# Cross-attention and quantised FFN on one core: one pass of scores with a block-transposed row maximum, and a new order of the attention step

## What is computed

```python
def xattn(q, kv, Wq, Wk, Wv, Wo, bo):        # 8 heads of 32
    qh, kh, vh = split_heads(q @ Wq), split_heads(kv @ Wk), split_heads(kv @ Wv)
    scores = einsum('bqhd,bkhd->bhqk', qh, kh) * 32 ** -0.5
    attn = softmax(scores, axis=-1)
    return merge_heads(einsum('bhqk,bkhd->bqhd', attn, vh)) @ Wo + bo

def ffn(x):                                   # weights rounded to -1, 0, 1, rows to 8 bits
    h = bitlinear(layernorm(x, g1, b1n), w1, b1)       # 256 -> 1024
    h = gelu(h, approximate=False)
    return bitlinear(layernorm(h, g2, b2n), w2, b2)    # 1024 -> 256

x = x + xattn(layernorm_plain(x), ctx_768, Wq, Wk, Wv, Wo, bo)
x = x + ffn(layernorm_plain(x))
```

## Time and profile before

| | |
|---|---|
| median of 3 runs | 1164.03 us (1163.67 to 1164.55) |
| the profiled execution | 1168.3 us, its span 1166.6 us |
| busy share of the span | TensorE 87%, its weight loads 63%, VectorE 88%, ScalarE 71%, GpSimd 60% |
| granted TensorE clock, mean | 0.982 |
| HBM | 90 GB/s over the span |

### The profile page before, as it was taken

How to read it: one execution, slowest core, us unless ns; L and a number is a source line. 1 busy time by engine, 2 the same in 40 slices (tenths; PEclk the granted TensorE clock), 3 DMA queues, 4 the chain that set the end, 5 groups by cost and what they waited for, 6 DMA issues and landing times.

```text
span 1166.6 us, 34313 instructions
## 1 busy us (share of the span) xinstructions
PE 1019.7 (87%) x12163; PEld 732.0 (63%) x12209; DVE 1024.2 (88%) x1589; ACT 833.6 (71%) x2147; POOL 701.0 (60%) x924
## 2 busy tenths in 40 slices
PE   5999999999999999999999876777777777777775
PEld 4777777777777777777777533444444444444444
DVE  1588989988888888888889899999999999999996
ACT  3555655676656666666665566999999999999993
POOL 3345555754545555555556546777777777777776
PEclk8999999999999999999999978999999999999997
DMA  5556867667788766676565400332222333333334
GB/s 140 138 144 158 151 148 153 146 144 144 152 141 131 162 147 151 144 143 142 142 141 121 115 25 19 37 37 36 36 36 36 36 36 37 36 36 38 38 37 68
DMA packets 144483, 114.30 MB, mean 98 GB/s; under 512 B 51580, under 2 KB 134908, under 8 KB 144408
## 3 DMA queue, kind: packets, MB, share of 16 engines
q1 hardware_dynamic: 126824, 96.38, 38.2%
q0 software_dynamic: 16864, 16.26, 11.7%
q10 hardware_dynamic: 720, 0.66, 0.2%
HBM read 71.23 MB, written 33.63 MB: 90 GB/s over the span
## 4 chain that ended last, share of the span: by engine, by line
PE 49%; DVE 23%; issue 20%; DMA 3%; ACT 2%; SPq 1%; POOL 1%; DVEq 1%; another core or an unknown queue 0%; ACTq 0%; POOLq 0%
PE banks L1317 8%; PE banks L1304 8%; DVE gn_low L797 6%; DVE gn_high L797 6%; PE banks L1236 6%; PE banks L1281 5%; PE banks L1247 5%; PE banks L1256 4%; PE banks L1267 3%; DMA r_rows<-x_r 2%; PE banks L1269 2%; DVE gn_high L783 2%; DVE gn_low L783 2%; PE banks L1295 2%; PE banks L1270 1%
## 5 line engine op out<-in xcount | busy, mean ns | idle before, releaser
L977 ACT ACTIVATE probs<-banks 120x512 f32<-120x512 f32 x256 | 132.2, 602 | 87.2 <-PE banks L1286 87.2
L517 POOL TENSOR_TENSOR f_r<-f_ve,neg_half 128x2 f32<-128x2 f32 x62 | 43.8, 707 | 211.9 <-DVE f_ve L734 210.3
L689 DVE TENSOR_REDUCE nm_part<-banks 128x16 f16<-128x1920 f32 x64 | 138.1, 2157 | 35.1 <-PE banks L1236 34.8
L1020 ACT ACTIVATE g_dev<-g,g_sum 128x1024 bf16<-128x1024 f32 x128 | 149.0, 1164 | 0.0
L1025 ACT ACTIVATE g<-banks,h_dq 128x1024 f32<-128x1024 f32 x128 | 142.5, 1130 | 8.4 <-PE banks L1183 8.4
L1201 PE MATMUL banks<-w_t,g_t 128*128 128x256 bf16 x1008 | 123.2, 276 | 13.5 <-ACT g_t L1052 10.9
L1317 PE MATMUL banks<-wo_sb,o_t 128*128 128x256 f32 x512 | 128.2, 394 | 5.8 <-DVE o_t L831 5.8
L1201 PEld LDWEIGHTS banks<-w_t,g_t 128*128 128x128 f16 x1008 | 94.7, 98 | 51.9 <-issue 30.3
L1304 PE MATMUL banks<-xt,wq_c 128*128 128x256 f32 x512 | 126.2, 389 | 0.6 <-issue 0.6
L1177 PE MATMUL banks<-w_t,h_t 128*128 128x512 bf16 x466 | 116.3, 385 | 5.5 <-ACT g L1025 1.9
L1317 PEld LDWEIGHTS banks<-wo_sb,o_t 128*128 128x128 f32 x512 | 94.4, 195 | 24.5 <-DVE o_t L831 6.2
(11 more groups left out here) (165 smaller groups left out, 2715.6 us busy)
## 6 DMA issues: line engine op xcount, KB each, us to landing
x_in<-in_x SPq DMA_DIRECT2D x64, 256.0 KB, 4.1
xt<-in_x_t SPq DMA_DIRECT2D x64, 256.0 KB, 3.7
xr<-in_x SPq DMA_DIRECT2D x64, 256.0 KB, 5.7
out<-xr SPq DMA_DIRECT2D x64, 256.0 KB
out<-res POOLq DMA_DIRECT2D x62, 256.0 KB, 4.4
r_bc<-r_rows SPq DMA_DIRECT2D x64, 128.0 KB, 4.8
ctx_t<-in_ctx_t SPq DMA_DIRECT2D x64, 120.0 KB, 3.2
w_raw<-in_w_t SPq DMA_DIRECT2D x8, 256.0 KB, 5.8
```

The lines of the kernel that those rows point to most:

```text
L689: dve.tensor_reduce(nm_part[:, q, :, 0:T * C], s_p, AX.X, ALU.max, negate=True).then_inc(max_done, 1)
L977: act.activation(probs[:, p, j, :, :], sc_p[:, j, :, :], ACT.Exp, scale=SCALE).then_inc(probs_done, 1)
L1020: act.activation(g_dev[:, t, :], g[:, p, t, :], ACT.Square, scale=-float(F), bias=g_sum[:, p, t:t + 1], accum_out=g_ssq[:, p, t:t + 1]).th ...
```

## The change

It touches the attention stage on all engines and the tail.

- `maxima` is gone. `scores(i)` is computed once, with the keys on the partitions, and no shift at first. The keys are padded from 120 to 128 by repeating eight of them (`KP`), so that all 128 partitions hold scores; only the first `KV = 120` go on.
- `largest(i)`: VectorE takes the negative maximum over transposed 32 by 32 blocks of all four banks (128 x 2048 in, 128 x 64 out). That leaves four partial maxima of each row, one for each 32 keys. `turn_minima` transposes them, VectorE takes the least of the four (`nm_row`) and spreads it over a block-diagonal tile (`nm_t`, 128 x 256).
- `shift(i)`: 8 products of 256 columns (f16) add the shift to the scores that still stand in the banks. ScalarE then takes the exponentials. ScalarE's copy of the minima is gone, and the exponentials come in two halves with `high_half` between them.
- The projection `y_p` moves from bank 0 to bank 2, which it shares with keys and queries; `project` runs a step later (block i-2).
- All four engines have a new order in the step; keys and values are copied at the start of ScalarE's step, and `q_t` stands before `o_t` at the end of VectorE's.
- All 64 steps run through `attn`, and the hand-written tail is shorter. The sum over the weights (`w2s_p`) moves to bank 3 and into step NB-2.

The core of the diff (semaphore and shape declarations, the tail of ScalarE and the input's padding are left out):

```diff
-        y_p = bank[0].rearrange("p (t n) -> p t n", t=T)
+        y_p = bank[2].rearrange("p (t n) -> p t n", t=T)
...
@@ VectorE
+                def largest(b):
+                    after(dve, nmt_ps, b)
+                    dve.wait_ge(raw_ps, b + 1)
+                    dve.tensor_reduce(nm_part[:, :, 0:C * RB], blocks_p, AX.X, ALU.max, negate=True,
+                                      apply_transpose=True).then_inc(max_done, 1)
...
+                    b = i - 3
+                    (f_r_done, h_centred; the two affine instructions, h_affine)
+                    if isinstance(i, int) and i == -1:
+                        largest(0)
+                    elif live(i, NB) and not (isinstance(i, int) and i == 0):
+                        largest(i)
+                    (h_max of block i-3)
+                    b = i
+                        dve.wait_ge(nmt_ps, b + 1)
+                        dve.tensor_reduce(nm_row[:, :], nmt_p.rearrange("p (k r) -> p r k", r=32), AX.X, ALU.min).then_inc(min_done, 1)
+                    (h_cl of block i-3)
+                        after(dve, sc_ps, b)
+                        dve.wait_ge(min_done, b + 1)
+                        dve.tensor_tensor(nm_t[:, :, :], nm_row[:, :].unsqueeze(1).to_broadcast([P, RB, 32]),
+                                          block_sel[:, :].unsqueeze(2).to_broadcast([P, RB, 32]), ALU.mult).then_inc(nmt_done, 1)
+                    (xr of i-2, h_qs of i-3, reciprocal of i-1, statistics of i-2, split of i-1,
+                     aggregate, centre with f_ve behind its first half, of i-2; q_t of i+2; o_t of i-1)
...
@@ ScalarE: attn(i, n)
+                    if live(i + 1, NB):
+                        copy_keys_values(i + 1, q, (n + 1) % 4)
+                    if live(i - 1, NB):
+                        copy_o(i - 1, q)
+                    (row sums and squares of block i + 4)
+                        exponentials(i, p, range(0, HC // 2))
+                        high_half(i - 1, q)
+                        exponentials(i, p, range(HC // 2, HC))
+                        cast_rows(i - 4, n % 4)
...
@@ TensorE
+                def scores(b, p):
+                    after(pe, probs_done, 4 * b)
+                    pe.wait_ge(q_done, b + 1)
+                    pe.wait_ge(k_done, b + 1)
+                    for c in range(C):
+                        for j in range(HC):
+                            last = pe.matmul(sc_p[:, j, c, :], k_t[strip(j), p, c, :], q_t[strip(j), p, c, :],
+                                             start=(c == 0), stop=False, skip_group_check=True)
+                    last.then_inc(raw_ps, 1)
+                def turn_minima(b):
+                    after(pe, o_done, b)
+                    pe.wait_ge(max_done, b + 1)
+                    pe.transpose(nmt_p, nm_part[:, :, :].rearrange("p j n -> p (j n)"), ident_h[:, :]).then_inc(nmt_ps, 1)
+                def shift(b):
+                    pe.wait_ge(nmt_done, b + 1)
+                    for c in range(C):
+                        for j in range(HC):
+                            last = pe.matmul(sc_p[:, j, c, :], head_sel[strip(j), c, :],
+                                             nm_t[strip(j), :, :].rearrange("p b r -> p (b r)"),
+                                             start=False, stop=(c == C - 1), skip_group_check=True)
+                    last.then_inc(sc_ps, 1)
...
                 def keys_values(b, p):
                     after(pe, q_done, b)
                     after(pe, v_done, b)
+                    (first product of the values)
+                    after(pe, x1_done, b - 3)
                     (products of the keys, rest of the values)
...
                 def attn(i, n):
-                    maxima(i + 1); values(i - 1); sums(i - 1); keys_values(i + 2); scores(i)
-                    spread_inverses(i - 1); queries(i + 2); turn_minima(i + 1); project(i - 1)
+                    scores(i); values(i - 1); project(i - 2); turn_minima(i); sums(i - 1); shift(i)
+                    keys_values(i + 2); queries(i + 2); spread_inverses(i - 1)
...
@@ tail
-                steps(dve, A0, NB - 1, L0, L1, attn, 4, aside)
-                affine_h(NB - 4); add_y(NB - 3); statistics(NB - 3); centre_h(NB - 3); invert(NB - 2); split(NB - 2); weigh(NB - 2)
-                centre(0); add_y(NB - 2); ffn(0); invert(NB - 1); statistics(NB - 2); split(NB - 1); affine_h(NB - 3); centre_h(NB - 2)
-                centre(1); weigh(NB - 1); ffn(1); add_y(NB - 1); statistics(NB - 1); affine_h(NB - 2); centre_h(NB - 1)
-                ffn(2); affine_h(NB - 1); ffn(3)
+                steps(dve, A0, NB, L0, L1, attn, 4, aside)
+                affine_h(NB - 3); invert(NB - 1); split(NB - 1); centre(0); add_y(NB - 2); weigh(NB - 1)
+                statistics(NB - 2); centre_h(NB - 2); ffn(0); centre(1); affine_h(NB - 2); add_y(NB - 1)
+                ffn(1); statistics(NB - 1); centre_h(NB - 1); ffn(2); affine_h(NB - 1); ffn(3)
```

More of the change, by code:

```diff
@@ L684, in attn @@
                         dve.tensor_tensor(xr[:, r2, :, :], y_p, xr[:, r2, :, :], ALU.add).then_inc(x1_done, 1)
[L685 removed]
+                    b = i - 3
                     if live(b, NB):
[L687 to L689 removed]
+                        dve.wait_ge(h_clipped, b + 1)
+                        dve.reciprocal(h_qs[:, q, :], h_cl[:, q, :]).then_inc(h_scaled, 1)
                     b = i - 1
@@ L724, in attn @@
                         last.then_inc(x1_aggr, 1)
+                        after(dve, hq_cast, b - 3)
+                        dve.wait_ge(x1_aggr, b + 1)
+                        for t in range(T):
+                            last = dve.scalar_tensor_tensor(out=h[:, r2, t, :], in0=xr[:, r2, t, :],
+                                                            scalar=f_mv[:, p, t, 0:1], in1=g1_bc[:, :],
+                                                            op0=ALU.subtract, op1=ALU.mult)
+                            if t == 0:
+                                dve.tensor_scalar(f_ve[:, p, :], f_mv[:, p, :, 1], 1.0 + LN_EPS, LN_EPS * LN_EPS,
+                                                  ALU.mult, ALU.add).then_inc(f_ve_done, 1)
+                        last.then_inc(h_centred, 1)
+                    b = i + 2
+                    if live(b, NB):
+                        after(dve, raw_ps, b - 1)
+                        dve.wait_ge(r_loaded[p], (b - p) * 8 + 16)
+                        dve.wait_ge(kvq_ps, b + 1)
+                        dve.tensor_tensor(q_t[:, p, :, :].rearrange("p m (t n) -> p m t n", t=T),
+                                          q_p.rearrange("p m (t n) -> p m t n", t=T),
+                                          r_bc[:, p, :].rearrange("p (n t) -> p t n", t=T).unsqueeze(1).to_broadcast([P, C, T, P]),
+                                          ALU.mult).then_inc(q_done, 1)
                     b = i - 1
@@ L741, in attn @@
-                    b = i - 2
-                    if live(b, NB):
-                        after(dve, hq_cast, b - 3)
-                        for t in range(T):
-                            last = dve.scalar_tensor_tensor(out=h[:, r2, t, :], in0=xr[:, r2, t, :],
-                                                            scalar=f_mv[:, p, t, 0:1], in1=g1_bc[:, :],
-                                                            op0=ALU.subtract, op1=ALU.mult)
-                            if t == 0 and live(i - 3, NB):
-                                after(dve, hq_done, i - 4)
-                                dve.wait_ge(h_maxed, i - 2)
-                                dve.tensor_scalar(h_cl[:, q, :], h_max[:, q, :], CLIP, 1.0 / QMAX,
-                                                  ALU.max, ALU.mult).then_inc(h_clipped, 1)
-                        last.then_inc(h_centred, 1)
```

324 lines of the change are left out of this document (128 added, 196 removed).

## The result

The changed kernel takes 1228.43 us (median of 4 runs, 1225.62 to 1232.08), the kernel before 1164.29 (4 runs) beside it: a ratio of 1.0553, interval 1.0524 to 1.0582. I forecast 1155 with a range of 1130 to 1184, so both the sign and the range were wrong. The profiled execution took 1227.72 us, its span is 1226.0, 59.4 over that of before, at a mean granted clock of 0.968.

The account below looks back on a forecast made before the run. A 9.72 us ring through TensorE and VectorE was to bound the changed attention step, before 9.98 by TensorE's queue. Gains of 1.8 (stage), 4.2 and 3.1 (tail), 9.1 in all, took 1164.0 to 1155 us; range 1130 to 1184.

Parts of the forecast that it names:

- the ring: Attention step: a closed chain of waits through VectorE and TensorE, 9.72 us once round, over both engines' floors.
- affine 0.88 (two of 0.48, overlapped): VectorE between `o_t` and the next block's maximum: the two affine instructions together take 0.88 us.
- forecast (629.6): Attention stage from first to last maximum: 629.6 us, before 631.4.
- has 1.7 us of cover: GpSimd's power for the affine part starts after `f_ve`; 1.7 us of VectorE work covers it.
- that rival: Maximum: the transposed read costs a second pass, maximum 4.4 us, ring 11.8, about 1285 us; chance 0.05.
- TensorE's floor 9.2: TensorE's own work in an attention step after the change: 9.2 us, or 8.9 if two tiling changes are free.
- VectorE's work of 9.1: VectorE's floor in an attention step: 8.4 us plus 0.13, 0.20 and 0.33, making 9.1.
- The ring is longer than its rows: Rival: hand-overs from maximum to shift cost more, each 0.1 us a step adding 6.3 us, kernel slower; chance 0.22.
- a ring of 10.25: Slower-kernel rival with upper bounds for maximum, least of four, `nm_t`, shift and turn: 10.25 us a step, 1185 us.
- the lower bounds of the maximum, the least of four and `nm_t`: Slack rival: three new VectorE costs at their lowest give a ring of 9.43 us, time 1137 us; chance 0.20.
- Rare work in full, 12.2 us: VectorE's rare instructions, formerly in its idle time, now stand inside the ring and count in full: 10.7 and 1.5 us.
- Tail to `centre`: 14.4 forecast: From the last maximum to the first `centre`: 14.4 us, before 18.6, a gain of 4.2.

Follow-up runs that it names:

- Experiment 1: The changed kernel with GpSimd's two additions held until VectorE's affine part of the same step is done: 1168.24 us, ratio to before 1.000.
- (2): The changed kernel with all of GpSimd's work in a step held until VectorE's affine part is done: 1206.47 us, ratio 1.032.
- (3): The kernel before, with GpSimd's additions held for VectorE's statistics so that they run beside the affine part: 1250.6 us, ratio 1.069.
- (7): The changed kernel with GpSimd's additions behind the affine part, and the maximum over only the first half of the heads: 1137.09 us.
- (6): The changed kernel with VectorE's maximum ahead of the affine part and GpSimd's additions first in a step: 1162.87 us, ratio 0.999.
- (10): The changed kernel with GpSimd's additions behind the affine part, eight rare VectorE instructions reading 32 elements, not 1024: 1154.43 us, ratio 0.992.
- experiment 5: The changed kernel with all GpSimd work behind the affine part, plus a 0.60 us VectorE reduction behind `o_t`: 1257.76 us.

## Why the prediction was wrong

**The step that failed** is one term of the ring: "affine 0.88 (two of 0.48, overlapped)". It was read from the earlier trace rows, the kernel before, where GpSimd stands idle while the affine part runs (in the step above from 455.10, the end of its second addition, to 458.69), and the change moves it next to GpSimd's additions. It measured 1.89. The ring with it is 9.72 + 1.01 = 10.73, the step to the hundredth. Experiment 1 takes that term back and nothing else, and the first-to-last stretch falls from 698.3 to 634.7 us (22.2 to 656.9). So 63.6 of the 68.7 us between forecast (629.6) and result go with this collision. Step by step, the affine pairs are longer by 53.8 us in sum, and the falls of the clock in seven steps, which kernel 1 lacks, make up some 10.5 more; uneven steps take 0.8 back. (By kernel 1's median, 4.7 us above its profiled execution, the share would be up to 5 smaller.) I had looked at GpSimd in that place, but only asked whether its power would be ready in time ("has 1.7 us of cover"), not what else it would be doing.

**The cause** is shown from three sides: taking the additions away restores the term (1), moving them moves the loss to the next vulnerable instruction (2), and making the overlap in the old kernel makes the loss there (3). That the shared port is the thing contended for is the Trainium skill's account; the runs show which operands suffer and by how much, not the port.

**What held.** The maximum at 2.29: 2.302, so a transposed read costs no second pass, and that rival is out. Least of four 0.20 net: 0.19. `nm_t` 0.42: 0.42. Shift 0.32: 0.33 (527.71 to 528.04). Keys and values 1.70: 1.70 (528.04 to 529.74). TensorE's floor 9.2: 9.25 (7). VectorE's work of 9.1 nearly held, but its floor did not: it was busy for 94.98 of 100 us, 10.19 of each 10.73, and without the 1.01 of the collision that is 9.18. To this come 0.24 of short stops between neighbours, as ahead of the split (529.79 to 529.92) and the centring (530.43 to 530.53), which I had put at nothing. So the wait ahead of `q_t`, forecast as 0.7, was 0.30, and the floor is 9.4 without contention (1) and 9.5 with some (6).

**The rivals.** "The ring is longer than its rows" had the right side and even the right kind, but its place was wrong: the stretch from maximum to shift measured 3.65 us (524.06 to 527.71), forecast 2.29 + 1.35 = 3.64. The loss lies one instruction earlier. No rival had an old instruction become slower by its new neighbour. Two sums of the rivals don't come out of their terms, and nothing hangs on them: a ring of 10.25 makes 1188 and not 1185 by the prediction's own 6.3 us for each 0.1, and the lower bounds of the maximum, the least of four and `nm_t` give a ring of 9.52 and not 9.43, since TensorE's path of 1.28 then counts.

**The rest of the sum.** Rare work in full, 12.2 us: the rule held (10), though kernel 1 shows 22 us above 63 steps of 9.72 (634.7 - 612.4), where I had 17 (629.6 - 612.4): the other 5 are the remaining miss in this stretch. Tail to `centre`: 14.4 forecast, 17.7 measured. In it lie these rows of TensorE and stretches of the table:

```profile
727.77 3.57 PE L1178 MATMUL banks<-w_t,h_t 128*128 128x512 bf16 x8 [0.72 <-ACT bias_st L1047]
731.27 1.03 PE L1184 MATMUL banks<-bias_mov,bias_st 6*128 6x512 bf16 x4
...
738.16 1.89 PE L1178 MATMUL banks<-w_t,h_t 128*128 128x512 bf16 x8
739.98 0.60 PE L1184 MATMUL banks<-bias_mov,bias_st 6*128 6x512 bf16 x4
```

```profile
728.00:732.00 4.00, 4.00 (x12) 1.04 (x10) 3.83 (x6) 0.92 (x2) 2.68 (x3) 0.50 0.26 64
...
736.00:740.00 4.00, 3.90 (x23) 2.25 (x24) 3.43 (x4) 3.43 (x9) 0.76 (x1) 1.00 0.01 2
```

The first FFN products run at a granted clock of 0.50, the lower level of 1.2 GHz, after TensorE had stood for 2.21 and 0.72 us: 3.50 us to the start of the bias products, against 1.82 for the next such group at a clock of 1.00, and 1.03 against 0.60 for the bias products. They also start 1.2 us after the exponentials, before 0.3, because `bias_st` now stands behind these on ScalarE. Together 3.0 of the 3.3 us missed. From the first `centre` on the gain was 6.2, forecast 3.1; why it was twice as large stays open.

**The hidden part of the answer.** Even without the collision the change wins nothing (1.000 in kernel 1). The steady step gains 0.26 us, 16 over the stage, but from the first to the last maximum kernel 1 takes 634.7 us and the kernel before 631.4: the rare work and the first steps take more than the gain, because the change spends the slack that hid them. The shorter tail gives some of it back, and by the medians nothing is left.

## What to carry to other kernels

When an instruction of VectorE is moved, look up what GpSimd does at its new place and at its old one: a duration from the trace holds only beside the neighbours that it had. In these runs instructions with two SBUF operands and a small `tensor_scalar` were the ones to keep away from GpSimd's additions; the maximum, which reads PSUM, and the reductions could lie beside them, so the long maximum is the place for GpSimd's bulk. And before adding up a ring, check what the slack that it removes was hiding: rare work, late loads and collisions all begin to count. So do the waits that the ring puts on TensorE: look at the granted clock, step by step.

## What was unexpected of the hardware

- An affine instruction of 128x256 with two SBUF operands took 0.47 alone and 1.49 beside GpSimd's additions of 128x512; a pair under a full overlap 2.91 in place of 0.88. The additions barely suffered: 1.27 alone, 1.30 to 1.45 beside it.
- A `tensor_scalar` on two elements a partition was held for 0.9 us (1.07 in place of 0.15), until the addition was over; in a late step of kernel 1 it was held for 0.66 in the same way.
- Each fall of the granted clock to 0.50 in the attention stage lasted 3.4 us and cost the step 1.5, in the changed kernel and in experiment 5.
- The 32 by 32 transposed maximum took 2302 ns for 2048 elements and 1240 for 1024, so 1.04 ns an element, the rate of a plain reduction.
